# Autocorrelation layer: the second spectra of key and value made by exchanging halves of the first with on-chip transfers

## What is computed

```
qf = fft(q, axis=L); kf = fft(k, axis=L)          # k = v = the context
corr = ifft(qf * conj(kf)).real                   # [L, D]
w, idx = top_k(corr over L, 9); w = softmax(w)
out = sum_i w_i * v[min(idx_i + pos, L-1)]        # a weighted sum of shifted copies of v
```

## Time and profile before

| | us |
|---|---|
| median of 3 runs (1369.1 to 1370.73) | 1370.2 |
| the profiled execution, whole | 1372.38 |
| its span | 1370.5 |
| PE busy in the span | 1130.3 (82%) |
| DVE busy | 1057.1 (77%) |
| ACT busy | 571.6 (42%) |
| POOL busy | 440.4 (32%) |
| mean granted TensorE clock | 0.917 of full |
| data moved by DMA | 95.52 MB, mean 70 GB/s |

### The profile page before, as it was taken

One profiled execution on the slowest core, in us unless ns is written; L12 is line 12 of the kernel. 1 busy time (PEld: TensorE's weight loads), 2 busy tenths in 40 slices (PEclk: granted clock), 3 DMA queues, 4 the chain that ended last, 5 costly groups with the idle time before them and its releaser, 6 DMA issues. The chain is left out here.

```text
span 1370.5 us, 24326 instructions
## 1 busy us (share of the span) xinstructions
PE 1130.3 (82%) x8176; PEld 847.3 (62%) x8176; DVE 1057.1 (77%) x3103; ACT 571.6 (42%) x1630; POOL 440.4 (32%) x556
## 2 busy tenths in 40 slices
PE   5779999999999999985599899998888886087183
PEld 4557777777777787764466666665565553066172
DVE  5676777777666676653488878888998976999998
ACT  3534444444444444442455555565444531311100
POOL 0313333333333333331333333333233210063094
PEclk9889999999999999996799999999889987588696
DMA  9311011111111111101311122111111210622012
GB/s 288 77 37 39 32 50 52 52 52 52 52 52 52 52 52 52 38 31 66 114 47 66 66 85 110 66 66 66 66 66 66 75 60 19 251 69 80 20 62 92
DMA packets 30958, 95.52 MB, mean 70 GB/s; under 512 B 4016, under 2 KB 10160, under 8 KB 30896
## 3 DMA queue, kind: packets, MB, share of 16 engines
q1 hardware_dynamic: 30896, 94.76, 20.0%
HBM read 64.34 MB, written 27.26 MB: 67 GB/s over the span
## 5 line engine op out<-in xcount | busy, mean ns | idle before, releaser
L585 POOL TENSOR_TENSOR prob_G<-prob_G,rl 128x512 f32<-128x512 f32 x96 | 99.9, 1041 | 289.8 <-DVE rl L492 289.8
L239 PE MATMUL ps_qkv<-w_hi,xT_hi 128*128 128x512 f32 x384 | 156.6, 408 | 21.3 <-DVE prob_G L497 9.2
L375 ACT ACTIVATE prob_G<-prob_G,negm 128x128 f32<-128x128 f32 x384 | 148.9, 389 | 59.3 <-DVE negm L435 59.3
L240 PE MATMUL ps_qkv<-w_lo,xT_hi 128*128 128x512 f32 x384 | 150.9, 393 | 0.0
L241 PE MATMUL ps_qkv<-w_hi,xT_lo 128*128 128x512 f32 x384 | 150.9, 393 | 0.0
L460 DVE TENSOR_TENSOR xT_lo<-ps_t,xT_hi 128x512 fp32r<-128x512 f32 x32 | 22.1, 692 | 125.8 <-ACT xT_hi L415 125.8
L901 PE MATMUL pair<-c_tw,c_mats 128*128 128x512 f32 x256 | 116.4, 598 | 1.6 <-DVE c_tw L1136 1.6
L313 PE MATMUL ps_qkv<-wo_hi,aT_hi 128*128 128x512 f32 x256 | 110.0, 430 | 0.0
L314 PE MATMUL ps_qkv<-wo_lo,aT_hi 128*128 128x512 f32 x256 | 102.6, 401 | 0.0
L315 PE MATMUL ps_qkv<-wo_hi,aT_lo 128*128 128x512 f32 x256 | 102.5, 400 | 0.0
L239 PEld LDWEIGHTS ps_qkv<-w_hi,xT_hi 128*128 128x128 f32 x384 | 72.9, 190 | 47.2 <-issue 24.5
(11 more groups left out here) (201 smaller groups left out, 2928.7 us busy)
## 6 DMA issues: line engine op xcount, KB each, us to landing
rows<-c_row SPq DMA_DIRECT2D x16, 640.0 KB, 3.6
xin<-in_x SPq DMA_DIRECT2D x16, 512.0 KB, 3.4
xres<-in_x SPq DMA_DIRECT2D x16, 512.0 KB, 5.0
x<-xres SPq DMA_DIRECT2D x16, 512.0 KB, 2.7
c_xin<-x SPq DMA_DIRECT2D x16, 512.0 KB, 5.5
c_cin<-in_ctx SPq DMA_DIRECT2D x16, 512.0 KB, 4.4
c_b_xres<-x SPq DMA_DIRECT2D x16, 512.0 KB, 5.9
m_late_row<-rows SPq DMA_DIRECT2D x10, 640.0 KB, 11.7
```

The costliest lines, as they stand in the source:

```text
L239: nc.tensor.matmul(ps_qkv[:, n, :], xT_hi[:, k, :], w_hi[:, k, cols], start=k == 0, stop=False)
L240: nc.tensor.matmul(ps_qkv[:, n, :], xT_hi[:, k, :], w_lo[:, k, cols], start=False, stop=False)
L375: r = nc.scalar.activation(prob(g)[:, j, :], prob(g)[:, j, :], ACT.Exp, bias=negm[:, h:h + 1], accum_out=lsum[:, h:h + 1])
L585: nc.gpsimd.tensor_tensor(prob(g), prob(g), rl[:, g * GROUP:(g + 1) * GROUP].rearrange("p (j o) -> p j o", o=1).to_broadcast([P, GROUP, T] ...
```

## The change

The constant matrices `b` and `ovb` (columns of the first transforms with their halves exchanged) go. PE makes only the first spectrum of key and value (`k_ps`, `v_ps` count one per sample), ACT copies only that one (`spec[.][0]`, `spec[.][2]`), and SP issues DMAs within the on-chip memory that write `spec[.][1]` and `spec[.][3]` from them: for the key rows 65 to 127 to rows 1 to 63, rows 0 to 63 to rows 64 to 127, and row 0 from the context's last position in HBM; for the value the two halves of 64 rows. New semaphores `kb_in` (three DMAs, 48 per sample) and `vb_in` (two, 32) are what DVE waits for ahead of `tq[1]` and of `products()`. SP's order becomes: `cin`, `xin`; wait `x2_done`; wait `k_done`, three DMAs; `xres`; wait `y_done`, store `rows`; wait `v_done`, two DMAs. The first load of constants has three matrices, of which two are split.

```diff
 # SP, body
-                if tail:
-                    sp.wait_ge(y_done, b - 1)
-                    sp.dma_start(rows[b - 2], row[par][:]).then_inc(row_out[par], 16)
                 if ahead:                       # cin, xin: unchanged
                     ...
+                if near:
+                    of, to = spec[1 - par][0], spec[1 - par][1]
+                    sp.wait_ge(k_done, c + 1)
+                    sp.dma_start(to[1:H, :], of[H + 1:T, :]).then_inc(kb_in, 16)
+                    sp.dma_start(to[H:T, :], of[0:H, :]).then_inc(kb_in, 16)
+                    sp.dma_start(to[0:1, :], ctx_in[c, T - 1:T, :]).then_inc(kb_in, 16)
+                if far:
                     sp.dma_start(xres[:], x1[b]).then_inc(xres_in, 16)
+                if tail:
+                    sp.wait_ge(y_done, b - 1)
+                    sp.wait_ge(fwd_in, 16)
+                    sp.dma_start(rows[b - 2], row[par][:]).then_inc(row_out[par], 16)
+                if near:
+                    of, to = spec[1 - par][2], spec[1 - par][3]
+                    sp.wait_ge(v_done, c + 1)
+                    sp.dma_start(to[0:H, :], of[H:T, :]).then_inc(vb_in, 16)
+                    sp.dma_start(to[H:T, :], of[0:H, :]).then_inc(vb_in, 16)
 # PE
-                if near:
-                    if far:
-                        pe.wait_ge(v_done, 2 * b + 2)
-                    split3(p_c, 1, c_hi[1 - par], c_lo[1 - par]).then_inc(k_ps, 1)
...
-                    if near:
-                        pe.wait_ge(k_done, 2 * c + 2)
                     spectrum(p_c, FWD_ODD, wT).then_inc(ws_ps, 1)
...
-                    split3(p_a, 2, c_hi[1 - par], c_lo[1 - par]).then_inc(v_ps, 1)
-                    split3(p_c, 3, c_hi[1 - par], c_lo[1 - par]).then_inc(v_ps, 1)
+                    split3(p_a, FWD_V, c_hi[1 - par], c_lo[1 - par]).then_inc(v_ps, 1)
 # ACT
-                if near:
-                    key_spectrum(1, f_c)
...
-                    for i, src in ((2, f_a), (3, f_c)):
-                        act.wait_ge(v_ps, 2 * c + i - 1)
-                        nc.scalar.activation(spec[1 - par][i][:], src, ACT.Copy).then_inc(v_done, 1)
+                    act.wait_ge(v_ps, c + 1)
+                    nc.scalar.activation(spec[1 - par][2][:], f_a, ACT.Copy).then_inc(v_done, 1)
 # DVE
-                                dve.wait_ge(v_done, 2 * b + 2)
+                                dve.wait_ge(vb_in, 32 * (b + 1))
...
-                        dve.wait_ge(k_done, 2 * c + i + 1)
+                        if i == 0:
+                            dve.wait_ge(k_done, c + 1)
+                        else:
+                            dve.wait_ge(kb_in, 48 * (c + 1))
                         nc.vector.tensor_tensor(tq[i][:], f_a, spec[1 - par][i][:], ALU.mult).then_inc(tq_done, 1)
```

More of the change, by code:

```diff
@@ L35 @@
 WO_SLOTS = 4
-FWD_A, FWD_ODD, INV_OUT, INV_CORR, N_DFT = 0, 4, 5, 9, 11
+FWD_A, FWD_V, FWD_ODD, INV_OUT, INV_CORR, N_DFT = 0, 1, 2, 3, 7, 9
 F32 = mybir.dt.float32
@@ L710, in autocorrelation_phase @@
         mats = sb("mats", [P, N_DFT, P])
-        fwd_hi = sb("fwd_hi", [P, 4, P], F32R)
-        fwd_lo = sb("fwd_lo", [P, 4, P], F32R)
+        fwd_hi = sb("fwd_hi", [P, 2, P], F32R)
+        fwd_lo = sb("fwd_lo", [P, 2, P], F32R)
         w24_sb = sb("w24_sb", [P, KD, NLOG])
@@ L781, in autocorrelation_phase @@
         k_ps = sem("k_ps"); k_done = sem("k_done"); v_ps = sem("v_ps"); v_done = sem("v_done")
+        kb_in = sem("kb_in"); vb_in = sem("vb_in")
         q_ps = sem("q_ps"); tq_done = sem("tq_done"); corr_ps = sem("corr_ps"); corr_done = sem("corr_done")
@@ L863, in body @@
             def body(b, par, near, far, last, tail, ahead):
-                if tail:
-                    sp.wait_ge(y_done, b - 1)
-                    sp.dma_start(rows[b - 2], row[par][:]).then_inc(row_out[par], 16)
+                c = b + 1
+                H = T // 2
                 if ahead:
@@ L913, in body @@
                     if far:
-                        pe.wait_ge(v_done, 2 * b + 1)
+                        pe.wait_ge(v_done, b + 1)
                     split3(p_a, FWD_A, xn_hi, xn_lo).then_inc(q_ps, 1)
@@ L945, in body @@
                     if near:
-                        pe.wait_ge(k_done, 2 * c + 1)
+                        pe.wait_ge(k_done, c + 1)
                     else:
                         pe.wait_ge(x2_done, 2 * b)
-                        pe.wait_ge(v_done, 2 * b + 2)
+                        pe.wait_ge(v_done, b + 1)
                     spectrum(p_b, FWD_A, wT).then_inc(ws_ps, 1)
-                    if near:
-                        pe.wait_ge(k_done, 2 * c + 2)
                     spectrum(p_c, FWD_ODD, wT).then_inc(ws_ps, 1)
@@ L990, in _ @@
             act.wait_ge(fwd_in, 16)
-            nc.scalar.activation(fwd_hi[:, :, :], mats[:, 0:4, :], ACT.Copy).then_inc(fwd_hi_done, 1)
+            nc.scalar.activation(fwd_hi[:, :, :], mats[:, 0:2, :], ACT.Copy).then_inc(fwd_hi_done, 1)
             def split_context(n, par):
@@ L995, in split_context @@
                 if later(n, 1):
-                    act.wait_ge(v_ps, 2 * (n - 1))
+                    act.wait_ge(v_ps, n - 1)
                 nc.scalar.activation(c_hi[par][:], cin[:], ACT.Copy).then_inc(chi_done, 1)
@@ L1020, in body, with key_spectrum @@
                 c = b + 1
-                def key_spectrum(i, src):
-                    act.wait_ge(k_ps, 2 * c + i + 1)
+                def key_spectrum():
+                    act.wait_ge(k_ps, c + 1)
                     if last:
                         act.wait_ge(tw_done, 4 * b)
-                    nc.scalar.activation(spec[1 - par][i][:], src, ACT.Copy).then_inc(k_done, 1)
+                    nc.scalar.activation(spec[1 - par][0][:], f_b, ACT.Copy).then_inc(k_done, 1)
                 if tail:
@@ L1031, in body @@
                 if near:
-                    key_spectrum(0, f_b)
+                    key_spectrum()
                 if tail:
@@ L1081, in _ @@
             dve.wait_ge(fwd_hi_done, 1)
-            nc.vector.tensor_tensor(fwd_lo[:, :, :], mats[:, 0:4, :], fwd_hi[:, :, :].bitcast(F32),
+            nc.vector.tensor_tensor(fwd_lo[:, :, :], mats[:, 0:2, :], fwd_hi[:, :, :].bitcast(F32),
                                     ALU.subtract).then_inc(fwd_lo_done, 1)
@@ L1269, in split_context @@
                 if later(n, 1):
-                    pool.wait_ge(v_ps, 2 * (n - 1))
+                    pool.wait_ge(v_ps, n - 1)
                 TT(c_lo[par][:], cin[:], c_hi[par][:].bitcast(F32), ALU.subtract).then_inc(clo_done, 1)
@@ L1661, in dft_matrices @@
     a[:, H] = (-1.0) ** t
-    b = np.concatenate([a[:, H:], a[:, :H]], 1)
-    b[:, 0] = t == T - 1
     o = np.concatenate([np.cos(odd), -np.sin(odd)], 1)
@@ L1666, in dft_matrices @@
     ov[T - 1] -= o.sum(0)
-    ovb = np.concatenate([ov[:, H:], ov[:, :H]], 1)
     c1 = 2 / T * np.concatenate([np.cos(even).T, np.cos(even).T], 0)
@@ L1675, in dft_matrices @@
     o3 = np.concatenate([-np.sin(odd).T, np.sin(odd).T], 0) / T
-    return np.stack([a, b, ov, ovb, o, c1 / 2, o1, o2, o3, c1, c2], 1).astype(np.float32)
+    return np.stack([a, ov, o, c1 / 2, o1, o2, o3, c1, c2], 1).astype(np.float32)
 def build(nc, x, ctx, wq, wk, wv, wo, w24, base, wb, gate, ident, causal, rope, dft, out):
```

## The result

The changed kernel takes 1403.53 us (median of 4 runs, 1399.18 to 1404.28); its time is 1.0236 times that of before, with a 95% interval of 1.0221 to 1.025. That is 33 us slower, where +9 were forecast (1379). The sign was right and the size was not, by a factor of almost four; the time lies above the range's upper end of 1398.

What follows compares the result with a forecast made beforehand. A DVE-PE-ACT cycle through xp, key spectra and tq[1] was taken to bound bodies, PE's work partly covering waits. From 1370.2: start +2.6, loop -1.6, clock +5.6 and +2.4, sum +9.0, so 1379 us, range 1366 to 1398.

Steps and rivals of the forecast that it cites:

- PE's and ACT's removed work at 0: Two products on PE and two copies on ACT per sample only fill waits, so removing them gains 0.
- the 35 to 42 that I named as a sign: Sign of being right: PE's busy time falls by some 35 to 42 us and the span doesn't.
- The value's transfers at 0: Value transfers start at 812.6, needed by tw at 824: 11 us of cover, cost 0.
- What is late next: Bodies 1 to 8: first tw (at most 0.5 to win) and logits (0.3) limit the gain; 0.2 each, -1.6.
- The landing: Last of three key DMAs lands 3.7 us after k_done, between 3.5 and 4.3, against 4.0 before tq[1] now.
- the 4.0 that I had named as a sign of being wrong: In DVE, tq[1] waiting past 4.0 us after k_done would show the forecast wrong.
- the prediction's own sum: Key transfers' landing after k_done: 0.1 + 1.2 for issues + 2.2 to 3.0 from issue to landing, 3.5 to 4.3.
- rival 3: Late key transfers land at 4.5 to 5, tq[1] waits in every body: 1393 us; chance 15%.
- the prediction's own rule: Landing is set against 4.0 in bodies 1 to 8; in 9 to 14 each 0.1 beyond 3.9 costs that much.
- Where no cover is: Key transfers exposed in body -1, +2.4, and body 0, +0.8; less splitting at the start -0.6, together +2.6.
- The clock: PE's new gaps lower the clock: +5.6 in bodies 1 to 8, +2.4 in bodies 9 to 14.
- my first rival: The clock falls no more than today, as work breaks up PE's gaps: 1371 us, no change; chance 20%.

Runs made afterwards that it cites:

- e3: Changed kernel, but the second query-key product reads the key's first spectrum and doesn't wait for the transfers, which all still run; 1371.01 us.
- e1: Changed kernel, but the key's second spectrum is made by product and copy as before, only the value's by transfers; 1372.57 us.
- h1: Like f1, but one key transfer of 128 rows, same 512 KB, replaces the two of 64, without exchange of halves; 1380.38 us.
- g3: Changed kernel with key copied and sent by column halves, 64-row transfers, HBM row later, first three samples by product, context and x1 loads early; 1366.85 us.
- f1: Changed kernel, but both key transfers have 64 rows and the single row from HBM is written later, with the value's transfers; 1393.3 us.
- h2: Like f1, but the first key transfer has 63 rows again; 1412.74 us.
- e4: Changed kernel, but PE still makes both removed products, into free banks that nobody reads; 1407.15 us.
- g1: Changed kernel, but the first three samples (bodies -1, 0 and 1) get the key's second spectrum by product and copy; 1388.5 us.
- h3: The same kernel as g3, measured again in five rounds on another chip; 1367.66 us, ratio 0.9981.

## Why the prediction was right and wrong

**PE's and ACT's removed work at 0: right from body 0 on, wrong in body -1 (see the clock).** PE starts at the same places relative to the others, with gaps of 1.11 and 1.17 where 1.2 was forecast, and e3 keeps both removals and takes the time of before. PE's busy time fell by 26.5 us, not by the 35 to 42 that I named as a sign. In a body without a fall it is 24.27 (748.18 to 777.95, below) against 26.26, 2.0 less where two products at 1.3 had been counted, and each fall of the clock gives 1.4 back (25.68 against 24.27).

**The value's transfers at 0: right.** e1 is 2.4 us over before, within 0.2% of it. Its loop is 1.6 us shorter, which is the one fall of the clock that before has there and e1 hasn't.

**What is late next: right.** The weights' spectrum takes over in e3 (14 times), h1 and g3. The loop's gain at a landing of 3.7 was put at -1.6 for eight bodies; h1, with 3.3, shows -2.2 for seven.

**The landing: wrong, the step that failed first.** I took 3.7 us between bounds of 3.5 and 4.3, from the `v_rel` rows, the only ones with three issues and on-chip at both ends. They measured 5.0 to 5.6, outside the bounds and past the 4.0 that I had named as a sign of being wrong. The first fault lies in how the rows were chosen: the window of the earlier trace rows holds 6 of the 48 transfers of `v_rel`, the last of them. All 48 in the trace of before:

```profile
DMA to landing us min/median/max: 2.2/4.0/4.9
```

With this median the prediction's own sum gives 0.1 + 1.2 + 4.0 = 5.3, between 3.5 and 6.2, and with it rival 3 would have been the forecast. That it meets the measured value may be luck, as the transfers of `v_rel` are smaller (32 to 96 KB) and run among other loads.

Two more assumptions were in it. The rows of `v_rel` "move less", as I wrote, and I let the 512 KB store stand for the bytes; but that is one transfer over all 128 partitions, and h1, its equal in rows and bytes, is indeed used after 3.3. Two halves take 1.2 more (f1), the odd count the rest (h2). The doubt had its place in rival 3 and I dismissed it with "4 us are 1.5 times what the 512 KB store needs", an argument from bytes against one from shape. From 5.2 the prediction's own rule follows closely: 5.2 - 4.0 = 1.2 in each of the loop's seven bodies is +8.4, with three more falls of 1.1 each (below) +11.7, measured +11.2; 5.2 - 3.9 = 1.3 in each of five Sinkhorn bodies is +6.5, measured +6.3. The split between lateness and clock in the first sum is less sure than its total: the loop's bodies without a fall take 29.7 to 29.8 us, before they took 28.2 to 28.3 in most cases, some 1.5 more each, and the four falls together add about 2.5, only 1.0 more than the single one of before.

**"Where no cover is": wrong, mis-sized as +3.2 (2.4 and 0.8), measured +16.1.** Three causes. The landing again: 4.8 and 5.9 for 3.7. Body 1 was left out: I costed two bodies without cover and took it for one of the loop, but before, `tq[1]` starts there 2.3 us after the release; now 7.3, +5.0. And body -1's wait leaves PE idle for 7.24 us, after which its products run at half the clock: the exposure in this body is 4.8 - 1.4 = 3.4, the body is 7.5 longer. Summed, 3.4 + 3.0 + 5.0 = 11.4 is late data. Of the other 4.7, some 4.1 are the clock in body -1: 6.53 - 3.81 = 2.7 at the correlation, and what is then left of the body, 7.5 - 3.4 - 2.7 = 1.4, goes with a second fall at the next query spectrum, ahead of which PE stands 3.90 us. The last 0.6, in body 0, isn't accounted for.

**The clock: wrong in cause and place.** I took +8.0 for falls brought by PE's new gaps in the loop and the Sinkhorn bodies. In the loop they bring none: e3 has the gaps and one fall, as before; e4 has no such gaps and six. There were falls all the same, together with the lateness that I had not forecast, worth 3.3 us at most where I had put 5.6; the Sinkhorn bodies' +6.3 is explained without any.

Where the gaps do bring falls is body -1, for which I had no clock term. Before, PE waits 2.46 us for `tq[1]` and 2.49 for the value's copy, and runs on at full clock:

```profile
669.53 3.81 PE L961 MATMUL pair<-c_mats,c_tq 128*128 128x128 f32 x32 [2.46 <-DVE c_tq L1187]
...
679.58 0.47 PE L889 MATMUL pair<-c_xn_hi,c_fwd_hi 128*128 128x512 f32 x1 [2.49 <-ACT c_spec L1075]
```

Without the key's product ahead of it the first wait is 3.67 (e3), without the value's the second is 3.89 (e1), and both are followed by work at half clock:

```profile
670.08 6.73 PE L971 MATMUL pair<-c_mats,c_tq 128*128 128x128 f32 x32 [3.67 <-DVE c_tq L1195]
```
```profile
679.08 0.77 PE L899 MATMUL pair<-c_xn_hi,c_fwd_hi 128*128 128x512 f32 x1 [3.89 <-ACT c_spec L1081]
```

This makes body -1 4.3 us longer in e3 (21.2 against 17.0), where nothing waits for a transfer, and 2.4 longer in e1, g1, g3 and h3, which is what these four still have in the head. In the changed kernel the late transfer alone is enough for the first of the two falls: e4, with both products in place, waits 5.86 us there and has it too. What a fall costs in the loop can be read from neighbouring bodies of the changed kernel (length, busy times, mean granted clock, DMA):

```profile
748.18:777.95 29.77, 24.27 (x112) 15.70 (x112) 23.59 (x75) 12.90 (x24) 10.01 (x16) 1.00 0.41 125
777.95:808.78 30.83, 25.68 (x112) 16.71 (x112) 23.55 (x75) 12.91 (x24) 10.68 (x19) 0.94 0.37 107
```

30.83 - 29.77 = 1.06, under the 1.4 I took and near the 1.24 of the earlier trace rows; two of the four falls cost only about 0.3. This is also the ground on which my first rival (the clock holds, 1371) and the forecast were told apart, and that question turned out to be the wrong one: with the landing at 3.7 or below the clock holds in the loop (h1, one fall as before). h1 comes out at 1380.4, next to the forecast 1379, but by other terms: +8.5 in the head, not +2.6, and nothing from the clock in the loop.

The rule of the Trainium skill on gaps that I quoted (page "TensorE: Matmul & The Clock Gate", section "HAM oscillation") would have no fall in e4 either, where the longest gap in a body of the loop is 2.09 us; the trace shows six falls. It holds for the loop's gaps that I feared, and not for the one that I did not foresee.

**The rivals.** Rival 3, late transfers, had 15% and 1393; its mechanism is the one that the runs show, e3 most directly. It decides from 3.9 to 4.0 us after the release. Its price was low for three reasons: 4.7 in place of 5.2, the head, and no link between lateness and clock (the 8.0 that it carried for the gaps hid this). The bounds of the landing should have come from all 48 rows of `v_rel`, with the upper one left open, as nothing in the trace of before had 64 partitions and 4 KB a row.

## What to carry to other kernels

A product on an engine that waits anyway costs next to nothing (and may, as in body -1, keep its clock up), so replacing it by a transfer can only lose, unless the transfer is provably there in time; measure the time from the release to the consumer's start before and hold the transfer's whole chain (issues, shape, what is in flight) against it, body by body, the first ones by themselves. Take the price of a transfer from all rows of its kind in the trace and not from one window, from the same shape and not only the same bytes, and where there is none, leave the bound open upwards. If such an exchange must be made, start it with the first half of the data that is ready, keep row counts at 64 or 128, and let the first steps, which have no cover, keep the product.
